# Steps with gelu: block transposes and diagonal copies of the probabilities ahead of gelu

## What is computed

```python
def attn_layer(x, Wqkv, qs, ksc, Wo):        # 16 heads of 64, windows of 32 tokens
    q, k, v = jnp.split(x @ Wqkv, 3, -1)
    q = l2norm(q) * qs                       # k likewise with ksc
    q = q * cos * scale + rotate_half(q) * sin * scale
    out = local_attention(q, k, v)           # softmax over own and previous window
    return out @ Wo
def ffn_layer(x, g, bln, W1, b1, W2, b2):
    a, gate = jnp.split(layernorm(x) * g + bln @ W1 + b1, 2, -1)   # 341 columns each
    return a * jax.nn.gelu(gate, approximate=False) @ W2 + b2
for i in range(6):
    x = attn_layer(shift_tokens(x), ...) + x
    x = ffn_layer(shift_tokens(x), ...) + x
```

## Time and profile before

| | us |
|---|---|
| median of 3 runs (3025.07 to 3029.13) | 3026.15 |
| the profiled execution | 3029.61 |
| its span in the trace | 3027.8 |
| TensorE busy | 2503.4 (83%) |
| VectorE busy | 2396.2 (79%) |
| ScalarE busy | 2024.5 (67%) |
| GpSimd busy | 1334.1 (44%) |

### The profile page before, as it was taken

How to read it: one execution, slowest core, us unless ns; L and a number is a source line. 1 busy time by engine, 2 the same in 40 slices (tenths; PEclk the granted TensorE clock), 3 DMA queues, 4 the chain that set the end, 5 groups by cost and what they waited for, 6 DMA issues and landing times. The chain is left out here.

```text
span 3027.8 us, 67036 instructions
## 1 busy us (share of the span) xinstructions
PE 2503.4 (83%) x28199; PEld 1515.7 (50%) x28199; DVE 2396.2 (79%) x2633; ACT 2024.5 (67%) x3592; POOL 1334.1 (44%) x894
## 2 busy tenths in 40 slices
PE   6999999999677887887888887888887888887875
PEld 3122222222355666666565666666655666655653
DVE  6998989987398877777877777877777877778873
ACT  1487878878566676667676667676666676666663
POOL 3111111110355565555655555655555655555650
PEclk7799999999889898888998889988898998888986
DMA  2123222221110010000100001000010001000000
GB/s 48 59 77 87 58 74 74 59 52 58 38 31 14 9 49 14 21 8 7 50 14 22 7 7 48 14 22 9 7 48 12 24 7 46 18 22 11 19 14 15
DMA packets 115169, 95.90 MB, mean 32 GB/s; under 512 B 72119, under 2 KB 89781, under 8 KB 114869
## 3 DMA queue, kind: packets, MB, share of 16 engines
q1 hardware_dynamic: 114516, 91.42, 11.1%
q10 hardware_dynamic: 352, 0.20, 0.0%
HBM read 57.83 MB, written 27.26 MB: 28 GB/s over the span
## 5 line engine op out<-in xcount | busy, mean ns | idle before, releaser
L613 ACT ACTIVATE PT<-E_ps 128x512 f32<-128x512 f32 x1024 | 534.5, 601 | 190.6 <-PE E_ps L1071 189.0
L812 DVE TENSOR_REDUCE mx<-S_ps 128x1 f32<-128x1024 f32 x512 | 601.4, 1218 | 33.1 <-PE S_ps L1062 27.6
L854 DVE TENSOR_REDUCE ss<-nrm 128x16 f32<-128x1024 f32 x192 | 231.2, 1215 | 218.7 <-ACT nrm L622 218.2
L1103 PE MATMUL W_ps<-w_qkv,x_cut 128*128 128x512 f32 x576 | 281.9, 489 | 127.3 <-DVE nrm L866 119.0
L551 POOL TENSOR_TENSOR pr<-pr,mxB 128x1024 f32<-128x1024 f32 x96 | 182.5, 1901 | 436.3 <-DVE mxB L927 435.1
L569 POOL TENSOR_TENSOR tc<-tc,ts 128x1024 f32<-128x1024 f32 x96 | 228.7, 2382 | 327.0 <-DVE ts L884 327.0
L1124 PE MATMUL T_ps<-ident,tc 128*128 128x128 f32 x1536 | 266.5, 301 | 121.5 <-POOL tc L569 52.6
L1136 PE MATMUL T_ps<-pT,v 128*64 128x128 f32 x3072 | 258.4, 321 | 118.5 <-ACT q_T L631 106.1
L1062 PE MATMUL S_ps<-KS,QS 48*128 48x512 bf16 x1024 | 328.3, 405 | 30.4 <-DVE mx L812 22.0
L1071 PE MATMUL E_ps<-QS,KS 64*128 64x512 bf16 x1024 | 319.5, 388 | 4.7 <-ACT PT L613 4.6
L567 POOL TENSOR_TENSOR tc<-nrm,rt 128x1024 f32<-128x1024 f32 x96 | 228.9, 2384 | 179.0 <-DVE nrm L866 179.0
(11 more groups left out here) (201 smaller groups left out, 5184.4 us busy)
## 6 DMA issues: line engine op xcount, KB each, us to landing
Wqkv_cut<-w_cut_b SPq DMA_DIRECT2D x72, 256.0 KB, 2.4
w_qkv<-Wqkv_cut SPq DMA_DIRECT2D x36, 512.0 KB, 4.5
rot<-in_rot SPq DMA_DIRECT2D x96, 128.0 KB, 2.5
w_raw_b<-in_Wqkv SPq DMA_DIRECT2D x36, 256.0 KB, 3.0
W_cut<-w_cut_b SPq DMA_DIRECT2D x24, 170.5 KB, 2.7
w<-W_cut SPq DMA_DIRECT2D x12, 341.0 KB
QS<-zp_q SPq DMA_DIRECT2D x96, 32.0 KB
w_o<-in_Wo SPq DMA_DIRECT2D x6, 512.0 KB, 4.2
```

The lines of the kernel that those rows point to most:

```text
L613: e.activation(m.PT[n % NPT][:, :], turns.bank("probs", n)[:, :], ACT.Exp).then_inc(turns.sem("probs", n), 1)
L812: e.tensor_reduce(m.mx[h % 2][:, i, hf:hf + 1], m.S_ps[n % 2][:, :, :], AX.XY, ALU.max).then_inc(s["sc_max"], 1)
L1103: e.matmul(bank, left[0], right[0], start=True, stop=False)
```

## The change

In `scalar_b` and in `vector_b` the condition `gelus` goes. `diagonals(u - 2)` and `blocks(u - 2)` then stand in every step where they stood in the steps without gelu. It concerns the 23 steps u = 8, 12, ..., 96.

```diff
@@ scalar_b
-        gelus = u >= 8 and u % 4 == 0
         r = m.rs[u % 2]
...
                          ACT.Copy).then_inc(turns.w_sem("v", u), 1)
-        if blk and not gelus:
+        if blk:
             diagonals(u - 2)
         c = mlp_chunk(u, 0)
...
             e.preload_act_table_set("natural_log_exp_and_others")
-        if blk and gelus:
-            diagonals(u - 2)
@@ vector_b
-        gelus = u >= 8 and u % 4 == 0
...
-        if blk and not gelus:
+        if blk:
             blocks(u - 2)
         if new:
             rotate(u)
...
-        if blk and gelus:
-            blocks(u - 2)
         if mid:
             score(u - 1)
```

## The result

| | median us | range |
|---|---|---|
| kernel before (4 runs) | 3027.64 | 3025.07 to 3034.2 |
| changed kernel (4 runs) | 3059.20 | 3055.02 to 3060.34 |

The ratio is 1.0098, with a 95% interval of 1.0079 to 1.0118: the change costs about 1%, 31.6 us by the medians, 29.8 us by the spans of the two profiled executions (3057.6 and 3027.8). The forecast was +13 us and slower, inside a range that holds the result; the size was less than half of what came.

A forecast was written before the change was run, and what follows sets the result against it. A chain passing between engines was taken to bound the kernel, ScalarE's order its late link. 1.1 + 2.2 - 2.7 = +0.6 us in 22 groups, +13 us, gave 3039 us; range 3000 to 3075.

The forecast's parts named there:

- The chain that sets the gelu step: Gelu step: copies ahead of gelus delay third up product, making TensorE's q projection the late link; +1.1 us at full clock.
- The half clock behind the gap: Gelu step, behind TensorE's 6.05 us idle: 4.5 us at half clock, half of it lost, +2.2 us (1.75 to 2.8).
- What is given back: Step behind gelu: full clock ends VectorE's wait for the down product; mean -2.7 us, -2.2 if a 0.54 wait stays.
- The sum: 1.1 + 2.2 - 2.7 = +0.6 us in each of 22 groups: +13 us.
- The last gelu step: u = 96: 7.87 us wait for the down product unchanged within a microsecond or two; taken as 0.
- First rival: Behind TensorE's gap, under 3.2 us of half clock makes the kernel faster; with none, 2991 us; chance 0.24.
- Second: Half clock behind the gap lasts 10.25 us, all 5.1 us of work double: +77, 3103 us; chance 0.14.
- Third: Table load between diagonals and gelus costs ScalarE up to 1.4 us more: 3069 us; chance 0.04.

The follow-up runs named there:

- the kernel with the small delay: Kernel before with 5 extra mask products on TensorE ahead of the third up product: 3029.40 us (ratio 1.0013).
- the one with the early transpose: Kernel before with only VectorE's block transpose moved ahead of the rotation, ScalarE's diagonal copies left behind the gelus: 2995.80 us (ratio 0.9898).

## Why the prediction was right in direction and short in size

- **The chain that sets the gelu step**: right. Copies at 1.00 us behind the copy of v, first gelu, `hid` and third up product in the walked order, TensorE idle 5.55 us (5.3 to 6.1 over the groups; 6.05 was said, but the v projection and output of this group ran partly at half clock and pushed the up products back), square of q released by the projection. With the gaps filled the order costs 1.00 us per group, where +1.1 was said.
- **The half clock behind the gap**: 4.85 us where 4.5 was taken, and a loss of 2.0 us (31.50 with it, 29.53 without) where 2.2 was said. The gelu step of 31.8 came out as 31.5.
- **What is given back**: right. -2.63 per group, -2.7 said; no wait at the sum of the down product; the same 19.15 when the clock was held in the kernel before.
- **The sum** is where it failed, by a term that it did not have. The sum stopped at the step behind gelu, as if the third and fourth step could not change. The third step has a gap of TensorE of its own, 2.80 us before and 2.79 now. The rows of 1736.00 in the earlier trace rows are that very gap, used there only as a sample for how long half clock lasts. The half clock there is now 6.70 us long, 6.00 of them behind the gap, instead of 3.50 or none: +1.11 us per group, 24 us in all. With it the sum is 2.96 - 2.63 + 1.11 + 0.08 = 1.52. The run that filled this gap alone took the kernel back to 3029.6.
- **The direction is in part luck.** The terms that the sum had come out as 2.96 - 2.63 = +0.33 us per group, 7 us, and the end of the kernel gave 3.0 of them back. By those terms alone the change would hardly be told from none. It is slower by the term that was left out, and the range holds the result although it was made from the half clock behind the long gap and the wait at line 955, of which neither came out near its upper end.
- **The last gelu step** was set at 0 within a microsecond or two; from the last normalisation to the end it gained 3.0 us. The down product at the end ran at full clock (2.82 us of down product at 3003.10 of its trace), and VectorE waited 1.95 us for it instead of the 7.87 of the earlier trace rows.
- **First rival** (the clock costs less than is gained): not so, since 4.85 us is above its point of 3.2. **Second** (10.25 us of half clock): the clock was back at 1714.90. **Third** (a dearer table load): the load takes 1.28 us and the first gelu starts 0.01 us behind it, at 1708.52. The Trainium skill, ScalarE: Activation LUTs, section "What ACT_TABLE_LOAD costs", puts a drain of about 1380 ns beside each load; the trace does not agree, in this place as little as in the one that was weighed.
- What stays open is why the third step's gap goes with 6.70 us of half clock in the changed kernel, with 3.50 or none in the kernel before. That it is the clock is shown. The traces show that the clock fell 0.7 us before TensorE came back in the one and 0.7 us after it in the other. That it turns on where the gap lies against the clock's last changes is what the kernel with the small delay suggests, in which the same instructions give four lengths; no run of its own shows it.

## What to carry to other kernels

Before moving work ahead of a chain that two engines pass back and forth, list what queues behind it on its engine and who waits for that: here eight copies of 0.65 us, whose results nobody wanted for some time, came to stand ahead of gelus that TensorE was waiting for. Where TensorE's clock falls in gaps, a sum by steps must go once round the whole period, since a change in one step decides how much half clock another gets; and a small gain or loss there says little about a change until the same comparison is made with the gaps filled. Filling two such gaps with products that nobody reads was worth more in this kernel (63 us) than the order under study (22 us).

## What the runs showed of the hardware that was not expected

- More work made the kernel faster. 16 extra bf16 products of 128x512 per group, in a gap of 3.83 us, took 44 us off 3025; 11 more in the third step took off another 18. The products themselves are short (two of them 0.60 us at full clock) and the stretch behind them keeps a granted clock of 1.00. The Trainium skill, TensorE: Matmul & The Clock Gate, section "HAM oscillation — how this bites in real kernels", describes a kernel whose TensorE waits for a DMA in every round and starts every round at the lower clock. Here the waits are for other engines, and the trace agrees: in the kernel before, a half-clock stretch of 10.25 us follows the gap of 3.83 us, and filling the gap takes it away.
- Periodic work and the clock fall into step. The kernel before alternates between groups of 90.2 and 90.7 us, the one with the early transpose sits at 88.75 in sixteen groups running, the one with the third up product delayed, its gelu step 0.3 us longer (28.85), goes round four lengths. A gelu step longer by 0.5 us went with a time shorter by 29 us in one kernel, and one longer by 0.3 us with no gain in another.
- Profiles of kernels that are the same up to u = 8 reach it between 952.0 and 963.4 us. Differences of less than 10 us between single executions are therefore better read per group than from the span.
